# Attention outputs with queries on partitions: the probabilities become the stationary operand, the values stream

## The reference

```
x = x + 0.5 * ffn(layernorm(x));  x = x + attn(layernorm(x));  x = x + 0.5 * ffn(layernorm(x))

def attn(x):                                   # 16 heads of 16, window 128, key/query 0 is global
    q, k, v = (x @ W.T).reshape(B, T, H, HD).transpose(0, 2, 1, 3)
    logits = einsum('bhqd,bhkd->bhqk', q, k) * 0.25
    logits = where(|q - k| <= 128 or q == 0 or k == 0, logits, -inf)
    out = einsum('bhqk,bhkd->bhqd', softmax(logits), v)
    return out.reshape(B, T, D) @ Wo.T
def ffn(tokens):                               # top 2 of 8 experts; an expert that gets more
    keep = counts <= capacity                  # than 1.25 * N / 8 tokens contributes nothing
```

## Time and profile before

| | |
|---|---|
| median of 3 runs | 983.21 us (979.47 to 1075.2) |
| the profiled execution | 983.19 us, span 981.4 us |
| instructions | 50638 |
| mean granted clock of TensorE | 0.967 of 2.4 GHz |

### The profile page before, as it was taken

How to read it: one execution, slowest core, us unless ns; L and a number is a source line. 1 busy time by engine, 2 the same in 40 slices (tenths; PEclk the granted TensorE clock), 3 DMA queues, 4 the chain that set the end, 5 groups by cost and what they waited for, 6 DMA issues and landing times.

```text
span 981.4 us, 50638 instructions
## 1 busy us (share of the span) xinstructions
PE 862.4 (88%) x21586; PEld 602.9 (61%) x21587; DVE 787.7 (80%) x2866; ACT 646.5 (66%) x1411; POOL 489.5 (50%) x812
## 2 busy tenths in 40 slices
PE   2788988899999989898999988898999989888892
PEld 1445655566667666666668666666667767565561
DVE  4379888998887789898877788997977788987674
ACT  2543767887767556797767656786776656778850
POOL 5211455665444546665544455664544445646751
PEclk9879999999999999999999999998999999999997
DMA  5221223242212333341212334341221333221031
GB/s 179 85 80 59 78 66 111 94 111 64 74 50 84 103 122 116 103 116 52 78 45 89 95 94 145 105 112 52 69 68 62 101 94 103 89 70 43 8 89 46
DMA packets 92518, 83.50 MB, mean 85 GB/s; under 512 B 17280, under 2 KB 91264, under 8 KB 92288
## 3 DMA queue, kind: packets, MB, share of 16 engines
q1 hardware_dynamic: 92288, 80.21, 25.8%
HBM read 20.65 MB, written 8.39 MB: 30 GB/s over the span
## 4 chain that ended last, share of the span: by engine, by line
PE 61%; DVE 20%; ACT 10%; issue 7%; POOL 1%; DMA 0%; SPq 0%; DVEq 0%; ACTq 0%; POOLq 0%
PE bank L936 11%; PE bank L893 11%; PE bank L789 10%; PE bank L918 9%; DVE bank L1346 7%; PE bank L803 5%; PE bank L773 5%; ACT probs L1046 4%; PE bank L955 3%; DVE attn L1398 2%; PE bank L706 2%; ACT pieces L1007 2%; ACT o_raw L1064 2%; DVE rest L1281 2%; DVE row_max L1346 2%
## 5 line engine op out<-in xcount | busy, mean ns | idle before, releaser
L1046 ACT ACTIVATE probs<-bank 128x384 f32<-128x384 f32 (+1 forms) x1024 | 466.0, 480 | 212.0 <-PE bank L918 205.0
L1346 DVE CUSTOM_DVE_ANT_0 bank<-bank,con 128x288 f32<-128x288 f32 x1024 | 497.4, 519 | 104.1 <-PE bank L893 95.2
L893 PE MATMUL bank<-k_stack,q_stack 96*32 96x288 bf16 x4096 | 322.0, 295 | 32.3 <-DVE row_max L1346 26.5
L918 PE MATMUL bank<-q_stack,k_stack 99*32 99x288 bf16 (+2 forms) x4096 | 316.0, 288 | 12.6 <-ACT probs L1046 10.0
L936 PE MATMUL bank<-probs,v_sb 128*32 128x128 f32 x5888 | 302.4, 276 | 2.0 <-ACT o_raw L1064 1.0
L1145 POOL TENSOR_SCALAR_AFFINE_SELECT probs<-probs 128x512 f32<-128x512 f32 x240 | 156.7, 653 | 228.8 <-ACT probs L1046 227.2
L936 PEld LDWEIGHTS bank<-probs,v_sb 128*32 128x32 f32 x5888 | 184.4, 112 | 40.8 <-issue 9.0
L893 PEld LDWEIGHTS bank<-k_stack,q_stack 96*32 96x32 bf16 x4096 | 119.5, 96 | 126.5 <-DVE row_max L1346 70.1
L1150 POOL TENSOR_SCALAR_AFFINE_SELECT probs<-probs 128x512 f32<-128x512 f32 x240 | 154.4, 643 | 30.2 <-ACT probs L1046 30.2
L789 PE MATMUL bank<-xnT,wqk_sb 128*32 128x256 f32 x2048 | 163.1, 395 | 0.7 <-ACT xnT L989 0.7
L918 PEld LDWEIGHTS bank<-q_stack,k_stack 99*32 99x32 bf16 x4096 | 118.9, 96 | 69.2 <-ACT probs L1046 46.5
(11 more groups left out here) (127 smaller groups left out, 744.8 us busy)
## 6 DMA issues: line engine op xcount, KB each, us to landing
q_stack<-pieces SPq DMA_DIRECT2D x384, 64.0 KB
k_stack<-pieces SPq DMA_DIRECT2D x384, 64.0 KB
x_ring<-in_x SPq DMA_DIRECT2D x28, 512.0 KB, 4.7
out_x<-x_ring SPq DMA_DIRECT2D x16, 512.0 KB, 3.5
attn<-in_x SPq DMA_DIRECT2D x4, 512.0 KB, 6.0
wback_sb<-in_wback SPq DMA_DIRECT2D x8, 256.0 KB, 6.0
q_stack<-neg_max SPq DMA_DIRECT2D x48, 16.0 KB, 2.2
probs<-in_wqk SPq DMA_DIRECT2D x1, 512.0 KB, 5.5
```

The lines of the kernel that those rows point to most:

```text
L893: last = pe.matmul(a_ring[i % len(a_ring)][SP * s:SP * (s + 1), 0:WIN], q_stack[g % 2][0:KROWS, h, q:q + SP], k_stack[g % 2][0:KROWS, h, q ...
L918: last = pe.matmul(b_ring[i % len(b_ring)][SP * s:SP * (s + 1), start:final], k_stack[g % 2][0:SROWS, h, WINDOW + P * j + SP * s:WINDOW + ...
L1046: act.activation(probs[:, j % 4, h, c0:c1], b_ring[i % len(b_ring)][:, c0:c1], ACT.Exp, scale=LOGIT_SCALE).then_inc(S["exp_ready"], 1)
L1346: dve.tensor_tensor_reduce(out=a_ring[i % len(a_ring)][:, 0:WIN], in0=a_ring[i % len(a_ring)][:, 0:WIN], in1=mask, scale=1.0, scalar=con[: ...
```

## The change

The operands of PV change places. `probs` is the stationary operand, 128 keys x 32 queries, in four strips of 32 queries; a head's 17 columns of `v_sb` stream. The output has queries on partitions and 4 items x 4 heads x 17 columns in `o_bank`. The products of one head over all its key tiles come together, heads spread over the quarters by `PV_QUARTERS`. COPY_OUT and TURN go. OUT is split in three events: the addition, reading `o_bank`, in quarter 3 of the step before; the reciprocal after that quarter's A; the multiplication stays after quarter 1's A of the next step, and now stands there alone. PE's next quartet waits for the addition; ACT's exponential of head h waits for the product of head h of the item that used the slot; PV waits once for the cuts of its last key tile. `v_sb` loses its padding, POOL its clearing.

```diff
-        v_sb = sb("v_sb", [P, NT, H * VW + SP - VW])
+        v_sb = sb("v_sb", [P, NT, H * VW])
-        LAG_TURN = LAG_PV + 4
+        LAG_OUT = LAG_PV + 4
+        O_COLS = HG * VW
+        PV_QUARTERS = ((1, 2, 3, 3), (0, 1, 2, 3), (0, 1, 2, 3), (0, 1, 2, 2))
@@ stages
-                    begin(LAG_TURN + NT * n + 4 * q, 0, "TURN", 4 * n + q)
-                    end(LAG_TURN + NT * n + 4 * q, 1, "OUT", 4 * n + q)
+                    opening(LAG_OUT + NT * n + 4 * q - 1, 3, "OUT_ADD", 4 * n + q)
+                    end(LAG_OUT + NT * n + 4 * q - 1, 3, "OUT_RECIP", 4 * n + q)
+                    end(LAG_OUT + NT * n + 4 * q, 1, "OUT_MULT", 4 * n + q)
@@ schedule
-                    if 0 <= pv < items and h < 3:
-                        if 0 <= pv % NT + h - 1 < NT:
-                            events.append(("PV", pv, h))
-                        if h == 2 and pv % 4 == 3:
-                            events.append(("COPY_OUT", pv // 4))
+                    if 0 <= pv < items:
+                        events += [("PV", pv, head) for head in range(HG) if PV_QUARTERS[pv % 4][head] == h]
@@ PE
-                            pe.wait_ge(S["band_ready"], band_count(NT * g + j))
-                            start, final = part == 0 or i == 0 and part == 1, part == 2 or j == NT - 1
-                            if start and n % 4 == 0 and n:
-                                pe.wait_ge(S["o_copied"], n // 4)
-                            for h in range(HG):
-                                head = HG * (g % NG) + h
-                                last = pe.matmul(
-                                    o_bank[SP * h:SP * (h + 1), P * (i % 4):P * (i % 4 + 1)],
-                                    v_sb[:, j, VW * head:VW * head + SP],
-                                    probs[:, j % 4, h, P * (i - j + 1):P * (i - j + 2)],
-                                    start=start, stop=final)
+                            keys = range(max(i - 1, 0), min(i + 2, NT))
+                            if h == 0:
...
+                                pe.wait_ge(S["band_ready"], band_count(NT * g + keys[-1]))
+                                if n % 4 == 0 and n:
+                                    pe.wait_ge(S["o_added"], n // 4)
+                            head = HG * (g % NG) + h
+                            to = O_COLS * (n % 4) + VW * h
+                            for j in keys:
+                                for s in range(4):
+                                    at = P * (i - j + 1) + SP * s
+                                    last = pe.matmul(
+                                        o_bank[SP * s:SP * (s + 1), to:to + VW],
+                                        probs[:, j % 4, h, at:at + SP],
+                                        v_sb[:, j, VW * head:VW * (head + 1)],
+                                        start=j == keys[0], stop=j == keys[-1])
                             last.then_inc(S["pv_done"], 1)
-                        elif kind == "TURN":
...
@@ ACT
-                            if n >= 4 and h == 0:
-                                act.wait_ge(S["pv_done"], pv_count(n - 3, 0))
+                            if n >= 4:
+                                act.wait_ge(S["pv_done"], HG * (n - 3) + h + 1)
-                        elif kind == "COPY_OUT":
...
-                            act.activation(o_raw[:, :], o_bank[:, :], ACT.Copy).then_inc(S["o_copied"], 1)
@@ DVE
+                        elif kind == "OUT_ADD":
+                            n, = n
+                            dve.wait_ge(S["pv_done"], 4 * HG * (n + 1))
+                            dve.wait_ge(S["glob_ready"], n + 1)
...
+                            dve.tensor_tensor(
+                                o_add[:, :, :, :].rearrange("p t h c -> p (t h c)"), o_bank[:, 0:4 * O_COLS],
+                                glob_term[:, :, :, :].rearrange("p t h c -> p (t h c)"), ALU.add)\
+                               .then_inc(S["o_added"], 1)
+                        elif kind == "OUT_RECIP":
...
+                            dve.reciprocal(recip[:, :, :], o_add[:, :, :, HD]).then_inc(S["recip_ready"], 1)
+                        elif kind == "OUT_MULT":
...
+                            dve.wait_ge(S["recip_ready"], n + 1)
...
```

More of the change, by code:

```diff
@@ L84, in build @@
         v0_all = sb("v0_all", [P, H * VW])
-        o_raw = sb("o_raw", [P, 4 * P])
         o_add = sb("o_add", [P, 4, HG, VW])
@@ L360, in band_count @@
             return g * (2 * NT - 2) + min(1 + 2 * j, 2 * NT - 2)
-        def pv_count(n, part):
-            g, i = divmod(n, NT)
-            return g * (3 * NT - 2) + min(3 * i + part, 3 * NT - 2)
         def window(j):
@@ L398, in stages @@
                     order.append((NT * NG * b - 20 + 4 * c if b else -16 + 2 * c, "EARLY", b, c))
-                    late = NT * NG * (b + 1) + (24 if b < nb - 1 else LAG_TURN - 15) + 4 * c
+                    late = NT * NG * (b + 1) + (24 if b < nb - 1 else LAG_OUT - 15) + 4 * c
                     order.append((late + 4, "LATE", b, c))
@@ L506, in schedule @@
                     events.append(("CUT", b))
-                q, turn = divmod(k + 3 - LAG_TURN, 4)
+                q, turn = divmod(k + 3 - LAG_OUT, 4)
                 if turn == 0 and 0 <= q < items // 4:
@@ L924, in _ @@
                         elif kind == "PV":
-                            n, part = n
+                            n, h = n
                             g, i = divmod(n, NT)
-                            j = i - 1 + part
-                            if g % NG == 0 and part == 2 and j % 2 == 0 or n % (NG * NT) == 0 and part == 1:
-                                pe.wait_ge(*emptied("VALUES", g // NG, j // 2))
-                            pe.wait_ge(S["band_ready"], band_count(NT * g + j))
-                            start, final = part == 0 or i == 0 and part == 1, part == 2 or j == NT - 1
@@ new lines, in _ @@
+                            if h == 0:
+                                if g % NG == 0 and (i == 0 or i % 2 == 1 and i + 1 < NT):
+                                    pe.wait_ge(*emptied("VALUES", g // NG, (i + 1) // 2))
+                                pe.wait_ge(S["band_ready"], band_count(NT * g + keys[-1]))
[3 more added lines that the diff above has]
+                            to = O_COLS * (n % 4) + VW * h
@@ L949, in _ @@
                             last.then_inc(S["counted"], 1)
-                        elif kind == "TURN":
-                            n, = n
-                            pe.wait_ge(S["o_copied"], n + 1)
-                            claim(pe, "TURN", n)
-                            for i in range(4):
-                                last = pe.transpose(bank_of("TURN", n)[:, P * i:P * (i + 1)],
-                                                    o_raw[:, P * i:P * (i + 1)], ident)
-                            last.then_inc(full_sem("TURN", n), 1)
                 @block.scalar
@@ L1058, in _ @@
                             act.activation(wide[1], wide[0], ACT.Exp).then_inc(S["route_exp"], 1)
-                        elif kind == "COPY_OUT":
-                            n, = n
-                            act.wait_ge(S["pv_done"], pv_count(4 * n + 3, 2))
-                            if n:
-                                act.wait_ge(*filled("TURN", n - 1))
-                            act.activation(o_raw[:, :], o_bank[:, :], ACT.Copy).then_inc(S["o_copied"], 1)
                 @block.gpsimd
@@ L1070, in _ @@
                         pool.wait_ge(S["k_ones"], 1)
-                    pool.memset(v_heads[:, :, :, HD], 1.0)
-                    pool.memset(v_sb[:, :, H * VW:], 0.0).then_inc(S["v_pads"], 1)
+                    pool.memset(v_heads[:, :, :, HD], 1.0).then_inc(S["v_ones"], 1)
                     for kind, *n in events:
@@ L1377, in _ @@
                             dve.memset(p0_arg[0:1, 1, :], MASKED).then_inc(S["p0_arg_ready"], 1)
-                        elif kind == "OUT":
+                        elif kind == "OUT_ADD":
+                            n, = n
+                            dve.wait_ge(S["pv_done"], 4 * HG * (n + 1))
+                            dve.wait_ge(S["glob_ready"], n + 1)
+                            if n:
+                                dve.wait_ge(S["attn_ready"], n)
+                            dve.tensor_tensor(
[3 more added lines that the diff above has]
+                        elif kind == "OUT_RECIP":
+                            n, = n
+                            dve.wait_ge(S["o_added"], n + 1)
+                            dve.reciprocal(recip[:, :, :], o_add[:, :, :, HD]).then_inc(S["recip_ready"], 1)
+                        elif kind == "OUT_MULT":
                             n, = n
@@ L1384, in _ @@
                                 dve.wait_ge(*filled("TURN_ATTN", late_index[g // NG - 1, quartet], 1))
-                            dve.wait_ge(*filled("TURN", n))
-                            dve.wait_ge(S["glob_ready"], n + 1)
-                            if n:
```

(10 more changed lines are left out.)

10 lines of the change are left out of this document (5 added, 5 removed).

## The result

The changed kernel takes 1,295.36 us in the median of four runs (1,288.62 to 1,298.96), beside 986.64 us for the kernel before in the same comparison: a ratio of 1.3153, 95% interval 1.3035 to 1.3271. (The ratio leaves out one run of the kernel before, of 1,075.2 us, which lay far above its other three.) It is 309 us slower where 14 us faster was forecast. The profiled execution took 1,292.28 us, its span is 1,290.2 us, its mean granted clock 0.883 (0.967 before).

The account below looks back on a forecast made before the run. No engine was full; PE, DVE and ACT took turns, PE holding 61% of the chain. Terms +24 - 34 - 10 - 12 + 12 + 2 - 1 + 5 = -14 us gave 969 us, range 942 to 1001.

Parts of the forecast that it names:

- instruction fetch: Delivery of PE's instructions: one packet in some 2.8 us, so PE should keep up; otherwise about 1010 us; chance 0.02.
- The product, +24: PV on PE: 23,552 small matmuls at 8.4 ns, 198 us, +36 us of PE, by chain share 0.67 +24 us.
- Turn -34: Transposes of the output on PE (L955) disappear: 29 us on the chain plus 5 for giving way, -34 us.
- copy -10: ACT's copy of the outputs (L1064) disappears, so piece 1 comes sooner: half of 20 us, -10 us.
- DVE's block -12: DVE's addition, reciprocal and multiplication become three pieces with a maximum between: -12 us, bounds 0 and -20.
- end -1: The end of the kernel loses a copy and a turn: -1 us.
- cuts +12: PV waits for POOL's cut of an item's last key: 17 to 20 us, on the chain +12 us.
- heads +2: ACT waits for the product head by head, mostly covered by pieces 1 and 2: +2 us.
- (a): New wait of PV on POOL's cuts, head 0 taking all keys early: 17 to 20 us, counted +12, bounds 0 and +29.
- (b): New wait of ACT's exponentials on each head's product, covered by pieces 1 and 2: +2 us, at most some 26.
- The clock, +5: PE's granted clock falls to half in five more quiet stretches, staying at 0.96 to 0.97: +5 us.
- clock case: Rival: thin streams drop PE's clock some 50 times, not 10, granted clock below 0.93: 1029 us; chance 0.12.

Follow-up runs that it names:

- bf16 product: Changed kernel with its product reading the upper halves of probabilities and values as bf16, one instruction pair per matmul instead of two: 987.33 us.
- kernel cut in thirds: Kernel before with each A and B matmul cut in three along its columns, old product, copy and turn kept: 1,249.93 us.
- one-column kernel: Changed kernel whose product streams only each head's column of ones instead of 17 columns, value columns left out: 1,316.27 us.
- bf16 pair: Changed kernel with bf16 probabilities and values by their upper halves, 986.55 us, beside kernel before with its product reading upper halves as bf16, 959.69 us.

## Why the prediction was wrong

**The step that failed** is the one on instruction fetch: "PE would take one packet in some 2.8 us, so it should keep up". It set 2.8 us, for which it gives no working, against the 1.2 us of a packet in the earlier trace rows. The packet's own time is only the middle of the cycle; 1.3 us before it and 1.4 us behind it are not in the DMA's rows, and transfers don't overlap. The cycle is 3.95 us in the median, no two transfers of the kernel after start less than 3.26 us apart, and PE needs a block every 3.2 us (983 / 306) to stay at the old time. The price of "about 1010" was wrong for the same reason. Two slips made it look safe: I laid the packets beside the instructions of all engines (50,638), where 171 x 256 shows that they are PE's alone; and I didn't read when they start. The trace of before has that: no two started less than 3.45 us apart, and the median was 5.37. With 80% more instructions 5.37 becomes 3.0, less than the 3.45, and so is the 2.8 itself: that was enough to see that they would not fit. The mechanism stood among the rivals, at 2%.

The Trainium skill, "Runtime: NRT & Kernel Launch", section "Instruction fetch mechanics", says that the sequencer fetches the next page of 256 instructions while the current one runs, so that crossing a boundary is mostly hidden. The traces agree on 256 and on one page ahead; they disagree on the cost where PE runs through a page in less than the cycle above, 3.95 us in the median: 319 us here.

**The product, +24.** The pace was right: 8 ns a matmul against 8.2 to 8.7, a head's 24 in 0.19 us. This is the duration on the array, and it was not what the product cost. Costed in instructions, 35,000 more of them, it is +330 (1,295 against 965 with the old product). The floor of about 25 ns from start to start in the Trainium skill, "TensorE: Matmul & The Clock Gate", section "Back-to-back issue gap", is contradicted once more, by these 8 ns.

**Turn -34, copy -10, DVE's block -12, end -1, cuts +12, heads +2** make -43 together. The old product in the new surroundings measured -15 to -27. What was mis-sized first is (a): PE waited 37 us on the cuts there and 39 with the bf16 product, not 17 to 20; at the 0.67 of the prediction that is +25 in place of +12. The rest, some 3 to 15 us, is spread over turn, copy and block. Only the block was tried alone, in the old surroundings: -4 to -10, within the bounds of 0 and -20 and short of 12, and there the multiplication met POOL (its cuts and its piece 3), which the prediction named as what would take this gain toward 0. In the kernel after the multiplication did get shorter (541 ns from 626). Head waits (b) were taken as covered: ACT waited 102 us for the product after, and 50 us with most of the pauses gone (also 50 with the old product; the kernel before has no such wait), above the 10 us that I named as a sign against the forecast. What that costs PE was not measured apart.

**The clock, +5.** Forecast 0.96 to 0.97, measured 0.883: 36 falls after 100 us with 288 us at half, against 10 and 47. By the prediction's own mark, below 0.93, this looks like the clock case; it is not. The kernel cut in thirds has 0.94 and loses 266 us, and the one-column kernel adds 345 us at half for 21 us of time. While PE waits for instructions, a slower array has idle time to spend. That the fall in the clock has no part in the 309 us isn't shown; that it isn't their main cause is. The mark was badly chosen: it couldn't tell a cause from a companion.

**The rest of the list.** DVE's wait for piece 1 is 15.7 us (under 15 forecast, 25.1 before), and 14.0 with the old product, so REST did come sooner. DVE is busy for 791 us (788). Exponentials that wait more than 10 us for the product were the sign of a wrong forecast, and they were there.

**Not settled:** what the 1.4 us between the end of a transfer and the next instruction are; whether other DMA traffic stretches the cycle (3.47 to 4.95 us); why a matmul of 64-wide strips takes 38 ns; and whether the exchange would gain anything if supply were no limit. In the bf16 pair it loses 27 us, but with 61 pauses still in the loser.

## What to carry to other kernels

Count PE's instructions before cutting matmuls smaller, both halves of every fp32 matmul and every weight load, and divide by 256: when the target time over the number of blocks comes near the spacing between instruction transfers in a dense stretch (3.95 us in the median here, 3.26 at the least), the array's pace no longer matters. An average somewhat above it isn't safe: at 4.2 us a block the dense stretches already cost 62 us. An idle "issue" gap between two instructions of one group that wait for nothing, at a constant count from the last such gap, is the sign. And a resource that is ruled out by its busy share must be priced by its whole cycle, with what lies ahead of and behind the transfer.

## What the hardware showed that was not expected

- PE's instructions come in blocks of 256, at most one ahead, and where each is run through at once they come 3.95 us apart in the median (3.93 in the kernel cut in thirds): a sustained 15 ns per instruction, while small matmuls run at 8 ns per matmul and its weight load, 4 ns an instruction.
- The loss is steep: 235 blocks +62 us, 299 blocks +266 us, 306 blocks (with all else that the change does) +309 us, against 171 before.
- Strips 64 wide took 38 ns a matmul where strips 32 wide took 8, and going from 32 to 64 wide or to the full array holds the group ahead for 0.23 to 0.24 us instead of 0.125.
- One streamed column in place of 17 took the granted clock from 0.883 to 0.752 (profiled runs; 0.782 to 0.891 in all four of the one, 0.767 in the second of the other), and the time went up by 21 us only, in a kernel bound by instruction supply.
- The same multiplication on DVE takes 420 to 424 ns where no POOL instruction overlaps it (in the kernels before, after and with the block taken apart) and 775 ns where POOL, by its recorded spans, overlaps more than 80% of it (with the block taken apart).
